# Second attention: one 128-row matmul per head instead of three block-diagonal products per four heads

## The reference

```python
q = (query @ w_q.T).reshape(B, T_q, 16, 32)
k = (kv_source @ w_k.T).reshape(B, T_kv, 16, 32)
attn = softmax(einsum('bqhd,bkhd->bhqk', q, k) * 32 ** -0.5)
out = einsum('bhqk,bkhd->bqhd', attn, v).reshape(B, T_q, 512) @ w_o.T
```

## Time and profile before

| | us |
|---|---|
| median of 3 executions | 1472.74 (1472.26 to 1474.9) |
| the profiled execution | 1471.78 |
| its span in the profile | 1469.7 |
| mean granted TensorE clock | 0.973 |
| PE busy | 1321.1 (90%) |
| DVE / ACT / POOL busy | 852.8 / 670.9 / 576.5 |
| scores of `attention1`, first to last | 323.9 to 728.2 |

### The profile page before, as it was taken

How to read it: one execution, slowest core, us unless ns; L and a number is a source line. 1 busy time by engine, 2 the same in 40 slices (tenths; PEclk the granted TensorE clock), 3 DMA queues, 4 the chain that set the end, 5 groups by cost and what they waited for, 6 DMA issues and landing times. The chain is left out here.

```text
span 1469.7 us, 27325 instructions
## 1 busy us (share of the span) xinstructions
PE 1321.1 (90%) x10010; PEld 797.8 (54%) x10010; DVE 852.8 (58%) x1726; ACT 670.9 (46%) x1890; POOL 576.5 (39%) x755
## 2 busy tenths in 40 slices
PE   6996666758999999999959999999999999899995
PEld 3544444436777777777634444444444444476663
DVE  5566999957888888887746655122221213354450
ACT  3332666628777777777723521111111112255552
POOL 1002688843354554545220004777700200145624
PEclk9997999989999999999979999999999999999998
DMA  6042000020011111111146103021120600268845
GB/s 232 29 172 87 1 1 2 1 87 17 9 45 59 45 52 52 45 59 59 45 143 67 29 1 87 1 59 32 27 59 0 215 1 29 94 171 188 210 57 72
DMA packets 85140, 96.99 MB, mean 66 GB/s; under 512 B 41968, under 2 KB 51344, under 8 KB 85008
## 3 DMA queue, kind: packets, MB, share of 16 engines
q1 hardware_dynamic: 67600, 73.04, 16.3%
q0 software_dynamic: 13248, 21.15, 7.7%
q10 hardware_dynamic: 4160, 1.05, 0.3%
HBM read 56.82 MB, written 38.45 MB: 65 GB/s over the span
## 5 line engine op out<-in xcount | busy, mean ns | idle before, releaser
L1406 DVE SCALAR_TENSOR_TENSOR shared_hf<-shared_ps_u,shared_sg 128x512 f32<-128x512 f32 x64 | 44.2, 691 | 275.6 <-PE shared_ps_u L105 261.2
L1133 POOL DMA_INDIRECT lists<-shared_load,shared_index x128 | 126.8, 991 | 167.6 <-DVE shared_sk L1274 126.3
L105 PE MATMUL shared_ps_g<-program_xs,program_wgu 128*128 128x512 f16 x768 | 178.7, 383 | 3.2 <-PEq L97 3.2
L896 ACT ACTIVATE attention_prob<-attention_ps_s,attention_nmax 128x120 f32<-128x120 f32 x512 | 177.2, 365 | 6.2 <-DVE attention_nmax L793 6.1
L1445 PE MATMUL shared_ps_y<-shared_wd,shared_hid 128*128 128x512 f16 x768 | 176.1, 379 | 2.0 <-DVE program_res L1432 2.0
L105 PE MATMUL shared_ps_u<-program_xs,program_wgu 128*128 128x512 f16 x768 | 176.7, 380 | 0.0
L1375 ACT ACTIVATE shared_sg<-shared_ps_g 128x512 f32<-128x512 f32 x64 | 38.2, 597 | 215.6 <-PE shared_ps_g L105 215.6
L1295 POOL DMA_INDIRECT program_x<-xn_rows,program_ex_slots x40 | 38.8, 969 | 243.6 <-PE experts_ps_x L1657 148.3
L105 PEld LDWEIGHTS shared_ps_g<-program_xs,program_wgu 128*128 128x128 f16 x768 | 75.6, 98 | 95.1 <-issue 6.1
L1445 PEld LDWEIGHTS shared_ps_y<-shared_wd,shared_hid 128*128 128x128 f16 x768 | 75.0, 98 | 92.8 <-DVE program_res L1432 2.4
L105 PEld LDWEIGHTS shared_ps_u<-program_xs,program_wgu 128*128 128x128 f16 x768 | 75.3, 98 | 91.3 <-issue 1.1
(11 more groups left out here) (276 smaller groups left out, 2565.4 us busy)
## 6 DMA issues: line engine op xcount, KB each, us to landing
xn_rows<-attention_g_xn SPq DMA_DIRECT2D x32, 256.0 KB, 2.3
xt_tiles<-attention_gT SPq DMA_DIRECT2D x32, 256.0 KB, 2.1
out_rows<-program_res SPq DMA_DIRECT2D x32, 256.0 KB, 2.1
program_xs<-xt_tiles SPq DMA_DIRECT2D x28, 256.0 KB, 5.0
program_x<-in_x SPq DMA_DIRECT2D x2, 3072.0 KB, 15.7
att_qr<-in_sh_guT SPq DMA_DIRECT2D x8, 512.0 KB, 4.1
program_x<-in_dyn_gT SPq DMA_DIRECT2D x8, 512.0 KB, 4.4
program_x<-in_dyn_uT SPq DMA_DIRECT2D x8, 512.0 KB, 5.5
```

Of the source, the lines that this page charges most:

```text
L105: last = pe.matmul(out, lhs(a, k), rhs(b, k), start=n == 0, stop=n == len(terms) - 1)
L896: last = act.activation(prob[:, c, h, :], ps_s[c % 2][:, h, :], ACT.Exp, bias=nmax[:, d % 2, c, h:h + 1], accum_out=rsum[:, d % 2, n:n + 1])
L1133: pool.indirect_dma_start(out=io["lists"], out_offset=bass.IndirectOffsetOnAxis(ap=index[:, t, k:k + 1], axis=0), in_=load[:, t, k, :], in ...
L1406: dve.scalar_tensor_tensor(hf[:, c % 2], ps_u[c % 2][:, :], HS / WS, sg[:, c % 2], ALU.mult, ALU.mult).then_inc(s["hf"], 1)
```

## The change

The scores are done by head. One matmul has 128 rows of contraction and covers all four products of parts of one head: rows 0 to 31 high query and high key, 32 to 63 high query and low key, 64 to 95 low query and high key, 96 to 127 low and low. It has 120 columns; a chunk c takes four of them, a tile sixteen. The operands stand in two new buffers, `g.queries` and `g.keys`, each with two slots; a head's 32 rows have to be carried from the partitions where `qT` and `k1` hold them to four places, which engines that work within a partition don't do. So SP issues DMAs inside SBUF: `spread` makes 4 x 4 = 16 of them (COPIES = 16) for a tile's queries and 16 for a batch's keys, each of 32 partitions x 4 pieces of 256 bytes (240 for keys), 32 KB in all.

- `kbd`, its zeroing and POOL's `block_keys` are gone; so are 12 matmuls of 480 columns a tile; 16 of 120 columns come in.
- All that leads to the queries runs one step earlier: queries of t+2 instead of t+1, transposes and `xT` of t+2, `ln.apply` of t+3, the statistics of t+6; LEAD is 6 instead of 5.
- `qT` has one slot instead of two. ACT writes the high part for the next tile only when the 16 DMAs of the tile before have landed (`q_in`).
- SP's step at a batch's first tile: `raw`, then the 16 DMAs of the next batch's keys, after the scores of the tiles before; in each step `xn_rows`, then the 16 of the queries of tile t+2, after its two splits and the scores of tile t; then `xt_tiles`.
- The first keys are carried at the end of `setup`. `simb` and `rs` move into the space of `queries`, which layer 0 doesn't need otherwise.

```diff
+COPIES = 4 * HC
+def spread(sp, to, parts, done):
+    for n, src in enumerate(parts):
+        for r in range(HC):
+            sp.dma_start(to[n * DH:(n + 1) * DH, r::HC, :], src[r * DH:(r + 1) * DH, :, :]).then_inc(done, 16)
+def packed_keys(sp, g, b):
+    cols = slice(b * J, (b + 1) * J)
+    hi, lo = g.k1[:, 0, :, cols], g.k1[:, 1, :, cols]
+    spread(sp, g.keys[:, b % 2], (hi, lo, hi, lo), g.keys_in[b % 2])
+def packed_queries(sp, g, u, qT, done):
+    spread(sp, g.queries[:, u % 2], (qT[:, 0], qT[:, 0], qT[:, 1], qT[:, 1]), done[u % 2])
...
-    LEAD, LAG = 5, 9
+    LEAD, LAG = 6, 9
-        qT = m.sb("qT", [P, 2, 2, KC, P], f16)
+        qT = m.sb("qT", [P, 2, KC, P], f16)
...
                         sp.dma_start(raw[:, :], io["sh_guT"][bass.ds(b * P, P), :]).then_inc(w_in, 16)
+                        if b + 1 < B:
+                            need(sp, c4["s_mm"], KC * t)
+                            packed_keys(sp, g, b + 1)
...
+                    u = t + 2
+                    if live(u):
+                        sp.wait_ge(s["q_hi"], u + 1)
+                        sp.wait_ge(s["q_lo"], u + 1)
+                        need(sp, c4["s_mm"], KC * (u - 1))
+                        packed_queries(sp, g, u, qT, q_in)
...
-                            need(act, c4["s_mm"], KC * (u - 1))
-                            act.activation(qT[:, q, 0], ps_q[:, :, :], ACT.Copy, scale=SC1 / WS).then_inc(s["q_hi"], 1)
+                            need(act, q_in[(u - 1) % 2], 16 * COPIES * ((u - 1) // 2 + 1))
+                            act.activation(qT[:, 0], ps_q[:, :, :], ACT.Copy, scale=SC1 / WS).then_inc(s["q_hi"], 1)
...
-                        pe.wait_ge(s["q_lo"], u + 1)
-                    if d == 0:
-                        pe.wait_ge(g.keys_ok, KC * HC * (u // TB) + HC * c + HC)
+                        pe.wait_ge(q_in[u % 2], 16 * COPIES * (u // 2 + 1))
+                    if c == 0 and d == 0:
+                        pe.wait_ge(g.keys_in[b % 2], 16 * COPIES * (b // 2 + 1))
                     need(pe, c4["exp"], KC * u + c - 1)
-                    matmuls(pe, ps_s[c % 2][:, :, :], lambda a, _: qT[:, d % 2, a, c, :], lambda a, _: g.kbd[:, a, c, :, :],
-                            ks=(0,)).then_inc(c4["s_mm"], 1)
+                    for h in range(HC):
+                        n = c * HC + h
+                        last = pe.matmul(ps_s[c % 2][:, h, :], g.queries[:, u % 2, n, :], g.keys[:, b % 2, n, :],
+                                         start=True, stop=True)
+                    last.then_inc(c4["s_mm"], 1)
```

More of the change, by code:

```diff
@@ L106, in matmuls @@
     return last
-def block_keys(pool, g, b, c):
-    for h in range(HC):
-        rows = slice(h * DH, (h + 1) * DH)
-        need(pool, g.keys_ok, HC * (KC * b + c) + h)
-        pool.tensor_copy(g.kbd[rows, :, c, h, :], g.k1[rows, :, c, bass.ds(b * J, J)]).then_inc(g.keys_ok, 1)
+def spread(sp, to, parts, done):
[8 more added lines that the diff above has]
+    spread(sp, g.queries[:, u % 2], (qT[:, 0], qT[:, 0], qT[:, 1], qT[:, 1]), done[u % 2])
 def setup(nc, g, io):
@@ L226, in _ @@
                 sp.dma_start(g.x[:, NT - 12:NT, :], xs[:, NT - 12:NT, :]).then_inc(x_in[1], 16)
+                sp.wait_ge(job_hi, last_job[3])
+                sp.wait_ge(job_lo, last_job[3])
+                packed_keys(sp, g, 0)
                 sp.wait_ge(job_mm, len(jobs))
@@ L240, in _ @@
                                    base=0, pattern=[[-1, P]], channel_multiplier=1).then_inc(id0, 1)
-                pool.memset(g.kbd[:, :, :, :, :], 0.0).then_inc(kbd_zero, 1)
-                pool.wait_ge(kbd_zero, 1)
-                pool.wait_ge(job_hi, 32)
-                pool.wait_ge(job_lo, 32)
-                for c in range(KC):
-                    block_keys(pool, g, 0, c)
-                pool.wait_ge(g.keys_ok, HC * KC)
             @block.scalar
@@ L699, in attention1 @@
         centred, xs_in = m.sem("centred"), m.sem("xs_in")
+        q_in = [m.sem(f"q_in{n}") for n in range(2)]
         rows_out = [m.sem(f"rows_out{n}") for n in range(2)]
@@ L756, in step @@
                 def step(t, d):
-                    u = t + 3
+                    u = t + 4
                     if live(u):
-                        ln.inverse_root(pool, g, u, (d + 3) % 4)
+                        ln.inverse_root(pool, g, u, d % 4)
                     u, q = t - 6, (d + 2) % 4
@@ L779, in step @@
                         pool.tensor_tensor(g.wgu[:, b, 1, :], raw[:, :], g.wgu[:, b, 0, :], ALU.subtract).then_inc(w_lo, 1)
-                    if live(t) and live(t + 1) and d == TB - 1:
-                        b = t // TB
-                        for c in range(KC):
-                            pool.wait_ge(c4["s_mm"], KC * t + c + 1)
-                            block_keys(pool, g, b + 1, c)
-                        pool.wait_ge(g.keys_ok, HC * KC * (b + 2))
                 run(pool, step)
@@ L849, in step @@
                         prob_low(t - 1, 2)
-                    if live(t + 5) or live(t + 4):
-                        ln.before(dve, t + 5)
+                    if live(t + 6) or live(t + 5):
+                        ln.before(dve, t + 6)
                     u, q = t - 2, d % 2
@@ L927, in step @@
                     if isinstance(t, int) and t == NT + 1:
-                        act.wait_ge(g.keys_ok, B * KC * HC)
+                        for n in range(2):
+                            act.wait_ge(g.keys_in[n], 16 * COPIES * B // 2)
                         tokens(act, g, io, 0, 0, xs_in)
@@ L1007, in step @@
                         outputs(t - 2, 3)
-                    u = t + 1
+                    u = t + 2
                     if live(u):
@@ L1013, in step @@
                         need(pe, s["g_lo"], t - 7)
-                        transposed(ps_x, ln.xn[:, (d + 1) % 2]).then_inc(s["xt_mm"], 1)
+                        transposed(ps_x, ln.xn[:, d % 2]).then_inc(s["xt_mm"], 1)
                     u = t - 3
@@ L1039, in step @@
                         need(pe, s["q_lo"], u)
-                        queries(u, d + 1, (0, 1))
+                        queries(u, d, (0, 1))
                     if live(t - 1):
@@ L1051, in step @@
                         pe.wait_ge(s["of"], u + 1)
-                        need(pe, s["xt_lo"], min(t + 2, NT) if isinstance(t, int) else t + 2)
+                        need(pe, s["xt_lo"], min(t + 3, NT))
                         need(pe, s["l_ok"], t - 7)
                         transposed(ps_x, of).then_inc(s["o_tr"], 1)
-                    u = t + 1
+                    u = t + 2
                     if live(u):
-                        queries(u, d + 1, (2, 3)).then_inc(s["q_mm"], 1)
+                        queries(u, d, (2, 3)).then_inc(s["q_mm"], 1)
                     if not past(t, 2):
@@ L1708, in program @@
         g.x_in = [m.sem(f"x_in{n}") for n in range(3)]
-        g.keys_ok = m.sem("keys_ok")
+        g.keys_in = [m.sem(f"keys_in{n}") for n in range(2)]
         io = dict(io, out=out)
@@ L1720, in program @@
             g.qr = a.sb("qr", [P, KC, D], bf16)
-            g.rs = a.sb("rs", [P, D])
-            g.kbd = a.sb("kbd", [P, 2, KC, HC, J], f16)
+            g.keys = a.sb("keys", [P, 2, HEADS, J], f16)
+            g.queries = a.sb("queries", [P, 2, HEADS, P], f16)
+            place = g.queries[:, :, :, :].rearrange("p s h n -> p (s h n)").bitcast(f32)
+            g.simb, g.rs = place[:, 0:JB], place[:, JB:JB + D]
             setup(nc, g, io)
```

27 lines of the change are left out of this document (14 added, 13 removed).

## The result

The kernel before takes 1472.54 us (median of 4 runs, 1472.26 to 1474.90), the changed one 1588.71 us (1587.94 to 1589.43): 1.0785 times as long, with a 95% interval of 1.0766 to 1.0804. It is 116 us slower. The forecast was 1478 us with a range of 1448 to 1504, and the result lies outside the range.

A forecast was written before the change was run, and what follows sets the result against it. PE was taken to bound the second attention. Its shorter steps saved time, but a start 17.7 us behind at tile 10 and stalls at the keys outweighed this: +5.2 us, forecast 1478 us, range 1448 to 1504.

The forecast's parts named there:

- What SP has to do instead: Second attention, SP's queue: sixteen DMAs inside SBUF per set at a pitch of 0.50 us, bounds 0.43 and 0.56.
- off by 0.02 or more: Sign that the forecast is wrong: SP's pitch within a set differs from 0.50 us by at least this.
- P: Time that sixteen DMAs of a set hold SP, taken as 8.0 us.
- S: Time from a set's first issue to its last landing: 15 x 0.50 + 1.9 = 9.4 us.
- The loop: Second attention, through the one `qT` slot: landings 9.4 plus 1.4 to DVE's low part, 10.8 us, hidden below 11.7.
- rival 2: SP issues slower, pitch 0.56: a loop of 11.7 to 11.8 us binds all steps, total 1504 us; chance 0.17.
- the forecast's chain: Second attention's start: low parts and landings followed tile by tile, leaving the stage 17.7 us behind at tile 10.
- Each 0.01 us of pitch is worth 4 us: Sensitivity of the total to SP's pitch, stated with faster issuing at 0.43; the other side begins below 0.487.
- the sum: Total of all terms against the profiled execution: +5.2 us, 1477.0 there, forecast 1478.
- the plain step: Second attention, a step without a batch's keys: 11.7 us where it was 13.14, laid out by hand.
- the stall at the keys: Second attention, once per batch: ACT waits 4.9 us because the next keys go out before the queries, nearly all stalling PE.
- rival 3: PE's clock falls in the stalls: seven stalls at 2 us each, +14, total 1491 us; chance 0.09.

The follow-up runs named there:

- experiment 5: Changed kernel with three products in 96 rows, 12 DMAs for a set instead of 16: 1499.25 us, ratio 1.0173 to the kernel before.
- experiment 4: Changed kernel with only one of the queries' sixteen DMAs issued from tile 2 on, keys' sets whole: 1608.14 us, ratio 0.9880 to the kernel before on that chip.
- experiments 1 and 3: 1: changed kernel, slots reordered so each DMA's pieces join, ratio 1.0645; 3: changed kernel, each set four 128-partition DMAs instead of sixteen, scores of wrong rows, ratio 0.9843.
- experiment 9: Bounce of queries and keys through device memory, with the keys' writes and first batch's reads moved from setup into the first attention: 1451.09 us, ratio 0.9869 to kernel before.

## Why the prediction was wrong

**The step that failed** is the pitch in "What SP has to do instead": "I take 0.50", with bounds of 0.43 and 0.56 from stores and loads that have one end in device memory. It measured 0.68 to 0.70, and "off by 0.02 or more" was the forecast's own sign of being wrong. The bounds were not bounds: none of the rows had both ends in SBUF, and the text says itself that no row shows such a DMA. By the forecast's own formulas, p = 0.685 gives P = 11.0 and S = 15 x 0.685 + 1.9 = 12.2, a loop of 13.6 us, and the trace shows 13.6 to 14.0 between plain sets. The loop is then above the step of 11.9 and binds all steps, which the text named as rival 2's mechanism. Run through with p = 0.685 and nothing else changed, the forecast's chain has tile 31's queries landed at 823, 104 us behind that tile's first chunk of scores in the kernel before (719.0). They landed at about 838, and the first chunk came at 839.4, 120 behind. So the pitch alone gives most of the loss. Most of the rest is in the batches, which take 65.5 us in the mean (349.79 to 742.98) where the chain gives 64. "Each 0.01 us of pitch is worth 4 us" was the slope on the near side; the forecast missed by 110 us for 0.185, 6 us for each 0.01, since past 0.56 the loop binds every step.

**What would have been wrong at the right pitch too.** In experiment 5 a set holds SP about as long as the forecast took, 7.7 to 9.1 us for 8.0, and the kernel is 26 us over the one before, where the sum says 5. A batch takes 54.4 us and not 51.7: the plain step is 11.9 and not 11.7 (11.94 in experiment 4, almost without the transfers), and the stall at the keys 6.8 and not 4.9. Over seven batches that is 19 us. These two terms were too small by themselves. In the changed kernel the plain step is not what binds, since the ring of 13.6 us is longer.

**What was right.** The chunk of scores takes 0.21 us, with the weight loads unseen: matmuls of 120 columns start at 489.26 and the next group at 489.47. By the 81 ns of the Trainium skill, TensorE: Matmul & The Clock Gate, Back-to-back issue gap, four would take an estimated 0.32 us; the trace decides for 0.21. Landing took 1.9 us, as taken. The start: scores 12.3 us later, 9.4 forecast plus nearly three for the pitch (15 x 0.185 = 2.8). Setup and the stages behind were not touched. PE didn't absorb the stalls: 63 us of its waits in 380 us are for queries.

**The clock** (rival 3, chance 0.09) did fall behind the stalls, to 0.67 in one stretch of 14 us. But PE is hardly on the path, which is SP's ring. The trace shows it for each tile: ACT's high part waits for a landing 31 times of 32, ACT's and DVE's writes take 0.60 and 0.69 us every time, and each set starts within 0.15 us of the end of DVE's write or, behind keys, of what stands ahead in SP's queue. PE comes onto the path only behind the last landing. There six matmuls take 2.45 us (from 837.08) where they take 1.46 at full clock, just ahead of tile 31's first chunk. So the clock has at most about 1 us of the 116.

**The store that POOL waits for** was missed. `xn_rows` stands behind the keys, and POOL's step waits up to 14.0 us for its landing. Whether it costs anything by itself was not tried; it is late by the same queue.

**Hold and landing.** The rows show the issuing engine held for 0.60 us by each DMA, while the data lands 1.9 us after the issue. The hold is a third as long as the landing, but it is paid one after another, and with sixteen in a row it is the larger part, 11 us against 1.9. The Trainium skill, DMA: Bandwidth & Descriptors, in its section Anatomy of one DMA, says of DMAs issued by GpSimd that a fixed cost of about 2 us is completion latency for the most part, with some 50 ns for the sequencer's dispatch and little for making the descriptors. These DMAs are issued by SyncE: their landing of 1.9 us is near those 2 us, and their hold of 0.60 us is far above 50 ns.

## What to carry to other kernels

Count the DMAs that a change adds to an issuing engine's queue per step and multiply by the time that the queue is held; bytes and latency come second. Take that time from a DMA of the same kind at both ends, and if the trace has none, let the range reach well past its neighbours and look for the value at which a hidden loop begins to bind. Where a rearrangement of partitions needs many transfers inside SBUF, one write to device memory and a few rearranging reads can be cheaper: 5 issues of 0.34 and 0.44 us here, against 16 of 0.68. And ask what stands ahead in the queue: most of the loss per batch came from the sixteen keys in front of the queries.

## What the hardware showed that I had not expected

- A DMA from SBUF to SBUF holds SP 585 to 601 ns at least and in the median (512 of 32 KB), 642 ns in the median for 128 KB, 0.59 after 10 us of pause. A read of as many pieces from device memory, each four times as large, holds it 432, a write of 256 KB 338. A store right behind one inside SBUF is held 0.59 where it was 0.32. What in the transfer causes it stays open; the layout of the pieces, the bytes and the partitions were excluded by experiments 1 and 3, a full queue by experiment 4. Whether another engine that issues them would be held as long was not tried.
- The eight writes of keys, of 240 KB in 1024 pieces of 240 bytes, held SP 2.2 us each in the median, and 21.4 us together, where a write of 256 KB of queries held it 0.34. Whether the small pieces do it, or the earlier writes that are still on their way (they land after 9.1 to 15.3 us), was not separated.
- Moving three times the traffic in that stage (its DMA share went from 0.14 to 0.43 of the time in the kernel of experiment 9) cost the engines nothing that the steps of 12 us would show.
